# A two-layer kernel: the products of a Mamba head pair regrouped, and its growth factors brought from HBM

## What is computed

```
proj = hidden_states @ in_proj_w                  # gate, x | B | C, dt
hbc  = silu(conv(x | B | C))
cum  = cumsum(dt * A)                             # per head, within a chunk
decay = exp(cum_i - cum_j), for i >= j
Y_diag = (C_i . B_j * decay * dt_j) x_j           # inside a chunk
states = sum_l exp(cum_last - cum_l) * dt_l * B_l x_l
prev   = scan over chunks: new = exp(cum_last) * prev + states
Y_off  = (C_l . prev) * exp(cum_l)                # from earlier chunks
hidden = (Y_diag + Y_off + D * x) * silu(gate), RMS norm, @ out_proj_w
```

## Time and profile before

| what | value |
|---|---|
| median of 3 runs | 1969.08 us (1966.39 to 1969.34) |
| the profiled execution, its own time | 1966.99 us |
| its span (first to last instruction) | 1965.2 us |
| mean granted matmul clock | 0.994 |
| matmul engine busy | 1911.9 us, 97% |
| VectorE, ScalarE, GpSimd busy | 78%, 67%, 42% |

### The profile page before, as it was taken

How to read it: one execution, slowest core, us unless ns; L and a number is a source line. 1 busy time by engine, 2 the same in 40 slices (tenths; PEclk the granted TensorE clock), 3 DMA queues, 4 the chain that set the end, 5 groups by cost and what they waited for, 6 DMA issues and landing times.

```text
span 1965.2 us, 43300 instructions
## 1 busy us (share of the span) xinstructions
PE 1911.9 (97%) x12642; PEld 1607.5 (82%) x12642; DVE 1532.6 (78%) x2860; ACT 1310.2 (67%) x2983; POOL 830.7 (42%) x997
## 2 busy tenths in 40 slices
PE   7999999999999999999999999999999999999998
PEld 7888778888888968888878886888888888788886
DVE  6886678888788468888878836888888883688886
ACT  4663389999555148888845514888875551588885
POOL 2210268888200016777710001777770000177776
PEclk9999999999999999999999999999999999999999
DMA  6330356656422114444422211544442221244442
GB/s 231 120 120 1 124 162 207 203 193 208 134 75 85 52 46 156 146 155 148 164 77 84 75 62 35 168 146 157 146 153 86 91 62 49 83 146 156 146 153 78
DMA packets 122051, 239.86 MB, mean 122 GB/s; under 512 B 10832, under 2 KB 48912, under 8 KB 121872
## 3 DMA queue, kind: packets, MB, share of 16 engines
q1 hardware_dynamic: 122000, 239.18, 37.2%
HBM read 198.37 MB, written 37.62 MB: 120 GB/s over the span
## 4 chain that ended last, share of the span: by engine, by line
PE 71%; issue 20%; DVE 5%; ACT 2%; POOL 1%; DMA 0%; POOLq 0%; DVEq 0%; ACTq 0%
PE bank L695 31%; PE bank L965 12%; PE bank L952 6%; PE bank L941 5%; PE bank L932 4%; PE bank L924 3%; PE both L695 2%; PE bank L845 2%; PE bank L802 2%; DVE conv_acc L1428 1%; PE both L802 1%; PE bank L772 1%; PE bank L777 1%; PE bank L854 0%; ACT bank L1166 0%
## 5 line engine op out<-in xcount | busy, mean ns | idle before, releaser
L695 PE MATMUL bank<-xn_r,w_r 128*128 128x512 f32 x2268 | 610.6, 409 | 4.2 <-issue 3.2
L695 PEld LDWEIGHTS bank<-xn_r,w_r 128*128 128x128 f32 x2268 | 413.1, 189 | 104.9 <-issue 27.2
L1428 DVE SCALAR_TENSOR_TENSOR conv_acc<-bank,conv_sb,conv_acc 128x511 f32<-128x511 f32 (+2 forms) x408 | 304.3, 746 | 39.0 <-ACT conv_acc L1161 5.3
L570 POOL TENSOR_TENSOR rstd<-var_eps,minus_half 128x4 f32<-128x4 f32 (+2 forms) x12 | 9.7, 808 | 627.9 <-DVE var_eps L1357 627.9
L965 PE MATMUL bank<-wo_n,place 128*128 128x256 f32 x1024 | 255.1, 392 | 1.6 <-DVE place L1606 1.6
L1344 DVE TENSOR_TENSOR place_r<-bank,place_r 128x512 fp32r<-128x512 f32 (+1 forms) x320 | 186.7, 632 | 76.2 <-ACT place_r L1084 76.2
L1084 ACT ACTIVATE place_r<-bank 128x512 fp32r<-128x512 f32 (+1 forms) x320 | 159.2, 556 | 126.0 <-PE bank L695 98.7
L591 POOL TENSOR_TENSOR shared<-shared,c_t 128x768 f32<-128x768 f32 x128 | 234.4, 1831 | 6.6 <-ACT shared L1262 6.6
L965 PEld LDWEIGHTS bank<-wo_n,place 128*128 128x128 f32 x1024 | 184.0, 189 | 43.2 <-issue 21.2
L613 POOL TENSOR_TENSOR sumsq<-sumsq,place 128x512 f32<-128x512 f32 x127 | 161.9, 1275 | 114.8 <-ACT place L1150 114.8
L695 PE MATMUL bank<-place_r 128*128 128x512 f32 (+3 forms) x960 | 188.9, 337 | 8.4 <-DVE place_r L1344 6.0
(11 more groups left out here) (163 smaller groups left out, 3597.0 us busy)
## 6 DMA issues: line engine op xcount, KB each, us to landing
place_r<-cum_rows SPq DMA_DIRECT2D x128, 512.0 KB, 3.9
w_r<-pair_split SPq DMA_DIRECT2D x96, 512.0 KB, 3.7
w_r<-qkv_split SPq DMA_DIRECT2D x48, 512.0 KB, 4.0
pair_split<-w_r SPq DMA_DIRECT2D x32, 512.0 KB, 4.0
qkv_split<-w_r SPq DMA_DIRECT2D x16, 768.0 KB, 3.9
w_r<-qkv_split SPq DMA_DIRECT2D x48, 256.0 KB, 3.2
wo_n<-out_split SPq DMA_DIRECT2D x96, 128.0 KB, 3.6
raw<-in_w_pair SPq DMA_DIRECT2D x32, 256.0 KB, 3.9
```

The lines of the kernel that those rows point to most:

```text
L695: ins = mm(out, lhsT=w(a), rhs=m(b), start=(start and i == 0), stop=(stop and i == 2), **kw)
L1428: stt(out=conv_acc[:, back:W], in0=src[:, 0:W - back], scalar=conv_sb[:, ch, TAPS - 1 - back:TAPS - back], in1=conv_acc[:, back:W], op0=AL ...
```

## The change

1. On the matmul engine a pair's products stand in another order: the six gate products of pair n + 1 and the six x products of pair n + 2 together, then turn_x of n + 1, project_out of n - 1, in_block of n, off_block of n, make_states of n + 1. turn_x puts all four transposes into bank 2, and weighted is one step of VectorE instead of two.
2. The states of a pair are made at the end of the pair before. GpSimd prepares them there (weigh_x, weigh_c of n + 1), after carry_states of n and add_squares of n - 1. The other engines' steps are reordered to match: ScalarE begins its pair with the copy of the states and conv_tanh, and in the first sequence does w_high for pair n + 3 in pair n; VectorE takes the taps of n + 2 at the end.
3. growth is gone from ScalarE. Once per sequence exp(cum) of all rows is formed in one step, saved to HBM (grow_rows, 0.13 MB), and per pair a transfer (grow_load, 128 x 2 x 384, 0.39 MB) brings it to all partitions, into c_grow, which now has a place of its own. It waits until off_block of two pairs earlier is done.

The core of the diff:

```diff
+            def grow_save(b):
+                sp.wait_ge(s_grow_ev, b + 1)
+                sp.dma_start(grow_rows[bass.ds(b, 1), :, :].rearrange("b h w -> h (b w)"), square[0:MH, :]).then_inc(s_grow_saved, 16)
+                sp.wait_ge(s_grow_saved, b * 16 + 16)
+
+            def grow_load(b, n, par):
+
+                if not first(b) or not isinstance(n, int) or n > 0:
+                    sp.wait_ge(s_off_done, b * NPAIR + n)
+                sp.dma_start(c_grow[:, par, :, :], grow_rows[bass.ds(b, 1), bass.ds(n * 2, 2), P:W]
+                             .to_broadcast([P, 2, W - P])).then_inc(grow_in[par], 16)
+
             def spread_load(b, n, par):
 
                 if isinstance(n, int) and n < 2:
                     sp.wait_ge(s_mix_exp, b * NPAIR + n + 1)
                 else:
-                    sp.wait_ge(s_grow_ev, b * NPAIR + n - 1)
+                    sp.wait_ge(s_span, b * NPAIR + n - 1)
...
+                pair_save(0, 0)
+                pair_load(2, 0)
                 for n in range(2):
-                    pair_save(n, n)
-                    pair_load(n + 2, n)
+                    grow_load(0, n + 1, 1 - n)
+                    pair_save(n + 1, 1 - n)
+                    pair_load(n + 3, 1 - n)
                     spread_load(0, n + 2, n)
                     out_load(n, n)
-                with sp.Fori(1, NPAIR // 2 - 1) as i:
+                with sp.Fori(1, NPAIR // 2 - 2) as i:
                     for par in range(2):
-                        pair_save(i * 2 + par, par)
-                        pair_load(i * 2 + par + 2, par)
+                        grow_load(0, i * 2 + par + 1, 1 - par)
+                        pair_save(i * 2 + par + 1, 1 - par)
+                        pair_load(i * 2 + par + 3, 1 - par)
                         spread_load(0, i * 2 + par + 2, par)
                         out_save(i * 2 + par - 2, par)
                         out_load(i * 2 + par, par)
-                for par in range(2):
-                    pair_save(NPAIR - 2 + par, par)
-                    out_save(NPAIR - 4 + par, par)
-                    out_load(NPAIR - 2 + par, par)
...
+                grow_save(b)
+                grow_load(b, 0, 0)
                 with sp.Fori(0, NPAIR // 2 - 1) as i:
                     for par in range(2):
                         sp.wait_ge(s_w_used, b * NPAIR + i * 2 + par + 1)
                         pair_fetch(i * 2 + par + 2, par)
                         spread_load(b, i * 2 + par + 2, par)
                         out_fetch(b, i * 2 + par, par)
+                        grow_load(b, i * 2 + par + 1, 1 - par)
...
             def weigh_c(b, n, par):
-                pool.wait_ge(s_grow_ev, b * NPAIR + n + 1)
+                pool.wait_ge(grow_in[par], (b * NPAIR + n - par + 2) * 8)
                 pool.tensor_tensor(c_grow[:, par, :, :], c_grow[:, par, :, :],
...
-                def pair(n, par, ahead, before=2):
-                    if before > 1:
-                        add_squares(b, n - 2)
+                def prepare(n, par):
                     weigh_x(b, n, par)
+                    weigh_c(b, n, par)
+
+                def pair(n, par, ahead, before=1):
+                    carry_states(b, n)
                     if ahead and first(b):
-                        split_low(NH + n + 2, par, 2 * D)
-                    weigh_c(b, n, par)
-                    carry_states(b, n)
+                        split_low(NH + n + 3, 1 - par, 2 * D)
+                    if before > 0:
+                        add_squares(b, n - 1)
+                    prepare(n + 1, 1 - par)
 
                 pool.wait_ge(s_dec_ready, b + 1)
+                if first(b):
+                    split_low(NH + 2, 0, 2 * D)
+                prepare(0, 0)
                 pair(0, 0, True, before=0)
...
             def turn_x(b, n, par):
                 N = b * NPAIR + n
                 pe.wait_ge(s_conv_silu, N + b * 2 + 4)
-                pe.wait_ge(s_gate_ready, N + 2)
-                for bk, t0 in ((0, 0), (2, 2)):
-                    for t in (t0, t0 + 1):
-                        ins = pe.transpose(bank[bk][:, t * P:(t + 1) * P], xs[:, par, t * P:(t + 1) * P], ident[:])
-                    ins.then_inc(s_x_turned, 1)
+                for t in range(NT):
+                    ins = pe.transpose(bank[2][:, t * P:(t + 1) * P], xs[:, par, t * P:(t + 1) * P], ident[:])
+                ins.then_inc(s_x_turned, 1)
...
-                    if before > 0:
-                        turn_x(b, n, par)
-                        off_block(b, n - 1, 1 - par)
-                    if not more and not last:
-                        pe.wait_ge(s_xdt_half, (b + 1) * NPAIR + 1)
+                    if more:
+                        project_gate(b, n + 1, 1 - par)
+                    elif not last:
+                        pe.wait_ge(s_gate_ready, (b + 1) * NPAIR + 1)
                         pe.wait_ge(s_taps_done, (b + 1) * (NPAIR + 2))
                         first_qk(b + 1)
+                    if ahead:
+                        project_x(b, n + 2, par)
                     if more:
-                        project_gate(b, n + 1, 1 - par)
-                    make_states(b, n, par)
-                    if before == 0:
+                        turn_x(b, n + 1, 1 - par)
+                    if before > 0:
+                        project_out(b, n - 1, 1 - par, isinstance(n, int) and n == 1, False)
+                    else:
                         pe.wait_ge(s_res_ready, b + 1)
                     in_block(b, n, par)
-                    if before > 0:
-                        project_out(b, n - 1, 1 - par, isinstance(n, int) and n == 1, False)
-                    if ahead:
-                        project_x(b, n + 2, par)
-
+                    off_block(b, n, par)
+                    if more:
+                        make_states(b, n + 1, 1 - par)
+
+                make_states(b, 0, 0)
...
                 act.wait_ge(s_hid_ready, N + 2)
                 act.wait_ge(s_summed, N + b + 1)
+                if isinstance(n, int) and n == 0:
+                    act.wait_ge(s_grow_saved, b * 16 + 16)
                 A(square, hid, ACT.Square).then_inc(s_squared, 1)
...
+                act.wait_ge(s_cum_ev, b + 1)
+                act.wait_ge(s_summed, b * (NPAIR + 1) + 1)
+                A(square, neg_cum, ACT.Exp, scale=-1.0).then_inc(s_grow_ev, 1)
...
-                def growth(n, par):
-
-                    A(c_grow[:, par, :, :], spread[:, par, :].rearrange("p (h w) -> p h w", h=2)[:, :, P:W], ACT.Exp,
-                      scale=-1.0).then_inc(s_grow_ev, 1)
...
+                def pair(n, par, more, ahead, deep, begin=False):
                     N = b * NPAIR + n
-                    if more and not begin:
-                        pair_conv_start(b, n + 1)
-                    if ahead and first(b):
-                        act.wait_ge(s_w_used, N + 1)
-                        w_high(NH + n + 2, par, 2 * D)
-                    elif not ahead and not last and par == 1:
-                        if first(b):
-                            act.wait_ge(s_gu_saved, 32)
-                        qk_high(b + 1, 0, copied=(b + 1) * 64)
-                    if more:
-                        if not begin:
-                            spans(n + 1, 1 - par)
-                        gate_tanh(b, n + 1, 1 - par)
                     act.wait_ge(s_state_done, N + 2)
                     act.wait_ge(s_off_done, N + 1)
                     copy_out(state[:].rearrange("p c q -> p (c q)"), bank[2][:, 0:W - P], s_state_ev)
                     if more:
-                        mixes(n + 1, 1 - par)
                         act.wait_ge(s_state_ev, N + 2)
                         conv_tanh(K + n + 3, bank[2])
-                        growth(n + 1, 1 - par)
                     if not begin:
                         squares(b, n - 1)
+                    if more:
+                        gate_tanh(b, n + 1, 1 - par)
+                        if deep and first(b):
+                            w_high(NH + n + 3, 1 - par, 2 * D)
+                        if ahead:
+                            pair_conv_start(b, n + 2)
+                        mixes(n + 1, 1 - par)
+                        if ahead:
+                            spans(n + 2, par)
+                    elif not last:
+                        if first(b):
+                            act.wait_ge(s_gu_saved, 32)
+                        qk_high(b + 1, 0, copied=(b + 1) * 64)
                     if first(b):
                         out_high(n, par)
...
-                for half, (bk, t0) in enumerate(((0, 0), (2, 2))):
-                    dve.wait_ge(s_x_turned, N * 2 + half + 1)
-                    tt(x_dt[:, par, t0:t0 + 2, :].rearrange("p t (h q) -> p t h q", h=2),
-                       bank[bk][:].rearrange("p (t h q) -> p t h q", t=NT, h=2)[:, t0:t0 + 2, :, :],
```

(25 more changed lines are left out.)

64 lines of the change are left out of this document (41 added, 23 removed).

## The result

| | us, median of the runs | ratio to before, 95% |
|---|---|---|
| before (5 runs) | 1967.22 | |
| after (5 runs, 1981.12 to 1990.90) | 1989.31 | 1.0102 [1.0081, 1.0124] |

The change made the kernel 1% slower (ratios and intervals here are taken over all executions, not from the medians), and 1989 us lies above the predicted range of 1944 to 1984. The profiled execution of after took 1990.2 us, its span is 1988.5 (before: 1965.2).

A forecast was written before the change was run, and what follows sets the result against it. The prediction took the matmul engine, busy for 97% of the span, as the bound. Terms of -32 us (sequences two to four) and +27 (first sequence) summed to -5, forecasting 1962.5 us, range 1944 to 1984.

The forecast's parts named there:

- a change of width costs 0.17 us: Matmul engine, pair loop: each change of tile width costs 0.17 us; four per pair become two.
- -32: Sequences two to four: pairs go from 7.81 to 7.47 us, in all -32 us.
- Rival C: Pair loop: width changes have no price, the 0.17 gaps are semaphore waits; time 1994 us; chance 0.06.
- no other engine takes over in sequences two to four: Pairs of 7.47 us stay bound by matmuls; VectorE needs 7.0, GpSimd and ScalarE have more room.
- Rival B: Sequences two to four: VectorE's waits cancel the gain while the first sequence still pays; 1994 us; chance 0.12.
- the loop's sum, 17.8 us: First sequence: off-diagonal products of n-1 to those of n+1 take 17.8 us, 8.9 a pair against 7.81.
- +27: First sequence: the loop through the queue's wait adds 27 us, from 1.09 in each of 28 pairs.
- growth issued to raw weights landed: First sequence's loop: time from issue of the growth transfer to landing of the raw weights, taken as 5.5 us.
- rival D: First sequence: landing over 6.3 us, DMA share above 0.7; +38 or more, 1973 to 1985 us; chance 0.14.
- the matmul engine's 7.3 us: First sequence's loop: products from states through off-diagonal, with one width change, take 7.3 us.
- the 3 us that I took off for start and end: First sequence: 3 x 0.34 at the end and about 2 at the start, deducted from 30.5 us.
- rival A: First sequence: the queue's wait does not bite, so all sequences gain, 42 us; 1925 us; chance 0.10.

The follow-up runs named there:

- experiment 4: The change with the state products of pair n+1 placed between the in-chunk and off-diagonal products of pair n: 2138.88 us, 1.0874 of before.
- Experiment 1: The change with the first sequence's growth transfer issued last in the queue's step, behind saving and loading of weights: 1927.84 us, 0.9804 of before.
- experiment 7: Experiment 1 with the weight save at the step's head waiting for the off-diagonal products of pair n-1: 1946.14 us, 0.9883 of before.
- 8: The change with GpSimd's sum of squares moved behind the weighting of x, in all sequences: 1973.01 us, 1.0028 of before.
- experiment 9: The change with four added 128-column products (0.9 us) per first-sequence pair, before the state products: 1986.93 us, 1.0108 of before.
- 3: The change with the growth transfer in the first sequence's loop cut from 384 to 8 columns per head: 1976.13 us, 1.0043 of before.
- 10: The change with eight added 128-column products (1.8 us) per first-sequence pair, before the state products: 1986.49 us, 1.0106 of before.
- experiments 5 and 6: The change with four, then ten, added 512-column products per first-sequence pair, before the state products: 2036.54 and 2189.92 us.

## Why the prediction was wrong, point by point

**Right: a change of width costs 0.17 us** and two of four go. Predicted -32, measured -31.2; experiment 4 gives 0.16 each. Rival C falls.

**Right: no other engine takes over in sequences two to four.** VectorE is busy for 195.61 of 224 us, so it idles 0.95 a pair, more than the 0.5 forecast; the DMA share is 0.61 (forecast about 0.6). Rival B falls. The exp per sequence and its trip through HBM cost nothing that shows.

**Right: the mechanism in the first sequence.** The growth transfer's wait at the head of the queue's step closes a loop over two pairs. Experiment 1 stretches it over three pairs (all gain comes back), 7 closes it over two again with the wait alone, 4 halves its span, 8 takes out one member.

**Wrong: the loop's sum, 17.8 us.** It was to give 8.9 a pair and +27; 9.61 and +54.9 were measured. The step that failed is the term "growth issued to raw weights landed", taken as 5.5. It measured 6.5: 1.5 until the load's issue as forecast, but 5.0 for the landing instead of 3.9. The 3.9 came from a kernel in which those transfers start with little ahead of them; right behind the growth transfer and the save it was 5.0, behind the save alone 3.5. I had nearly this value, 6.3, as rival D's threshold, and gave D 0.14 because I looked for a DMA share above 0.7; the share was 0.63. By its own sign, a landing later than 6.3 us after the growth issue, D came true. By these runs what counts is what stands ahead in the burst that the wait releases, not the share of the whole stretch: experiment 7 has a share of 0.73 and the 3.5. This is 0.5 a pair, 28 x 0.5 = 14 us.

**Missing: the clock.** The prediction took the matmul engine's 7.3 us at full clock although its own loop held waits of 2 x (8.9 - 7.47) = 2.9 us a turn for that engine; they came mostly as one of about 3.3. Nine falls followed: by experiment 9 some 10 us, at 1.6 us each 14.

**The rest:** 54.9 - 27 - 14 leaves 14 us, and the clock takes 10 to 14 of them. Two smaller errors stand against each other. The last step of the sequence took 12.64 us for 9.19, and the 3 us that I took off for start and end weren't there: +6. The steps from the landing to the state products take 4.2 us where nothing waits, against 4.52 in the sum (the two hand-overs and the 0.2 were too much): 28 x 0.18 = -5. No experiment takes these two apart.

The sum of signs was the weak place: -32 was known to 1 us, +27 hung on a landing time whose error counts half in each of 28 pairs. The ends given for it (+23 and +38) nearly covered the late landing (6.3 for 6.5), but not the clock.

**The better version** is experiment 1: the change with one line of the queue moved, 1927.84 us, 0.9804 [0.9787, 0.9820] of before. It is what rival A described (1925), and shows that the loss lay in the order of one queue.

## What to carry to other kernels

When a transfer with a new wait joins an in-order queue, put it behind everything in its step that is ready earlier, and follow what stands behind it to the engine that sets the pace: if the chain comes back to the wait, its whole length, over the pairs it spans, is the new period. Take landing times for such a chain from transfers that start in a burst, not from the median of a stretch where they start apart. If the chain makes the matmul engine wait 2 to 4 us at a time, allow for products that then run at half clock: here nine of 13 waits of 2.4 us and more were followed by it.

## What was unexpected of the hardware

- The half-clock stretches in the pairs came behind single waits of 2.2 to 3.7 us in the change and in experiments 3, 8 and 9, and behind 2.9 to 5.4 us in experiment 4; in experiment 7, with waits up to 1.9 us, and in 10 there was none. The length of the wait does not decide alone: in the change 3.45 us passed without a fall, in experiment 9 a fall came behind 2.36.
- A full fp32 product of 512 columns with a 128-wide tile shows as two records, one every 0.43 us (eight in 3.70 us, overlapping); the projections of the same width (fp32r) have one each, every 0.23. That is what spoilt experiments 5 and 6.
- The gap at the change from L1004 to L991 reads 0.33 on the weight loads and the one at L971 0.17, together 0.50, while by the pairs' times two changes of width cost 0.33: the marks on weight loads are no measure of what each one costs.
